# Two programs joined into one: cross-attention's first tile inside the tail of self-attention, and the third V product after the second gather group

## The reference

```python
x = layernorm(x + attn(x, W_qkv, b_qkv))
# cross-attention: K and V of the context, sums over pairs, level by level
Ks.append(0.5 * (k2[:, :, :, 0] + k2[:, :, :, 1]));  Vs.append(v2[:, :, :, 0] + v2[:, :, :, 1])
nk, nv = flatK[:, :, idx_table], flatV[:, :, idx_table]        # 12 nodes for every row
w = softmax(concat([Q.K_own, where(mask, -inf, Q.nk)]) * scale)
out = (w * concat([V_own, nv])).sum() @ Wo.T + bo
x = layernorm(x + out)
x = layernorm(x + relu(x @ w1 + b1) @ w2 + b2)
```

## Time and profile before

| | us |
|---|---|
| median of three runs | 2318.53 (2316.12 to 2335.72) |
| the profiled execution | 2324.6 |
| its span | 2322.5 |

### The profile page before, as it was taken

One profiled execution on the slowest core, in us unless ns is written; L12 is line 12 of the kernel. 1 busy time (PEld: TensorE's weight loads), 2 busy tenths in 40 slices (PEclk: granted clock), 3 DMA queues, 4 the chain that ended last, 5 costly groups with the idle time before them and its releaser, 6 DMA issues.

```text
span 2322.5 us, 34454 instructions
## 1 busy us (share of the span) xinstructions
PE 1981.8 (85%) x11744; PEld 1037.3 (45%) x11744; DVE 1846.2 (79%) x2416; ACT 1056.7 (45%) x1854; POOL 1115.6 (48%) x1132
## 2 busy tenths in 40 slices
PE   6599999999899999983248988989888899889997
PEld 2244344344344444421015555555555555555555
DVE  8489788888788998783678988888888888988850
ACT  3255555555555555552113444444444444444444
POOL 4234555544354645352536555556555456455420
PEclk9799999999999999996569999999999999999999
DMA  5334344435445443320966576666576566676520
GB/s 195 111 119 133 118 137 130 132 113 155 128 128 155 128 145 114 124 87 26 367 236 209 193 242 213 204 236 220 196 246 209 200 244 202 207 253 201 203 83 19
DMA packets 188808, 392.50 MB, mean 169 GB/s; under 512 B 20692, under 2 KB 82260, under 8 KB 188632
## 3 DMA queue, kind: packets, MB, share of 16 engines
q1 hardware_dynamic: 133336, 188.91, 25.5%
q0 software_dynamic: 55296, 201.35, 25.2%
HBM read 312.33 MB, written 77.59 MB: 168 GB/s over the span
## 4 chain that ended last, share of the span: by engine, by line
DVE 28%; DMA 10%; issue 6%; PE 4%; POOL 4%; SPq 1%; ACT 0%; DVEq 0%; ACTq 0%; POOLq 0%
DMA nb<-kv_flat,idx_rows 9%; DVE bank L1564 7%; DVE logits L1511 6%; DVE nb L1502 5%; DVE nb L1560 4%; POOL nb L1635 4%; PE bank L1239 2%; PE bank L1215 1%; DMA own<-kv_flat 1%; DVE bank L1570 1%; DVE logits L1515 1%; DVE own L1506 1%; SPq L1134 1%; DVE top L1533 1%; DVE total L1541 1%
## 5 line engine op out<-in xcount | busy, mean ns | idle before, releaser
L1635 POOL DMA_INDIRECT nb<-kv_flat,idx_rows x384 | 366.2, 954 | 137.7 <-issue 93.0
L761 DVE TENSOR_REDUCE neg_max<-rows_ps 128x1 f32<-128x512 f32 x512 | 327.0, 681 | 94.8 <-PE rows_ps L533 91.5
L1502 DVE TENSOR_TENSOR nb<-nb,bank 128x1024 f32<-128x1024 f32 x192 | 231.2, 1218 | 133.5 <-DMA nb<-kv_flat,idx_rows 118.7
L676 ACT ACTIVATE probsT<-e_ps 128x1024 f32<-128x1024 f32 x256 | 261.7, 1022 | 74.1 <-PE e_ps L565 74.0
L1663 POOL TENSOR_TENSOR nb<-nb,weights 128x1024 f32<-128x1024 f32 x96 | 182.5, 1914 | 233.2 <-DVE weights L1548 232.5
L1564 DVE TENSOR_TENSOR bank<-bank,nb 128x512 f32<-128x512 f32 x384 | 268.3, 699 | 25.1 <-DVE bank L1564 0.9
L1215 PE MATMUL bank<-x2T_hi,w_hi_sb 128*128 128x256 f16 x1024 | 280.8, 274 | 2.6 <-issue 2.6
L1215 PE MATMUL bank<-x2T_lo,w_hi_sb 128*128 128x256 f16 x1024 | 280.7, 274 | 1.5 <-issue 1.5
L1215 PE MATMUL bank<-x2T_hi,w_lo_sb 128*128 128x256 f16 x1024 | 280.5, 274 | 0.6 <-issue 0.4
L802 DVE TENSOR_TENSOR probsT<-probsT 128x2048 f32<-128x2048 f32 x96 | 229.3, 2388 | 13.7 <-ACT probsT L676 13.7
L1418 ACT ACTIVATE hid_hi<-bank,b_down 128x256 f16<-128x256 f32 x256 | 120.6, 471 | 246.0 <-remote 127.2
(11 more groups left out here) (163 smaller groups left out, 3808.7 us busy)
## 6 DMA issues: line engine op xcount, KB each, us to landing
kv_flat<-kv_nat SPq DMA_DIRECT2D x128, 256.0 KB, 2.7
own<-kv_flat SPq DMA_DIRECT2D x32, 512.0 KB
q_stack<-qk_dram SPq DMA_DIRECT2D x96, 128.0 KB, 2.8
k_stack<-qk_dram SPq DMA_DIRECT2D x96, 128.0 KB, 3.1
piece<-in_pieces SPq DMA_DIRECT2D x40, 256.0 KB, 3.0
in_sb<-in_xT SPq DMA_DIRECT2D x8, 1024.0 KB, 6.4
in_sb<-in_ctxT SPq DMA_DIRECT2D x8, 1024.0 KB, 7.8
qk_dram<-hi SPq DMA_DIRECT2D x32, 256.0 KB, 2.2
```

The source lines that it names most:

```text
L676: act.activation(probsT[:, PROBS_PLACE[quad % 2][kt], side:side + 2, :], e_ps[:], ACT.Exp, scale=1.0 / (Q_UP * K_UP)).then_inc(e_done, 1)
L761: dve.tensor_reduce(neg_max[:, g % 2, at + i:at + i + 1], rows_ps[:, i, :], AX.X, ALU.max, negate=True).then_inc(max_done, 1)
L1502: dve.tensor_tensor(kk, kk, q.unsqueeze(1).to_broadcast([P, GN, D]), ALU.mult)\
L1635: pool.indirect_dma_start(nb[:, slot(lt, g), k, :], None, kv_flat, bass.IndirectOffsetOnAxis(idx_rows[:, lt, at:at + 1], 0))\
```

## The change

There is one program, with one list of semaphores, all raised at its start. The buffers of the second part lie over those of the first that are no longer used (the function `over` makes several views of one buffer), and the PSUM banks are shared out anew. The helpers of the second part (key_sums, shift, normalise, values, gather, weight_values and so on) are the same, but for the bank's name (ROW for O) and what is shown below. What the second program did at its start is put into steps of the last batch (cross_early, called in every step of the eighth iteration) and of the tail (cross_late):

- last batch, SyncE at step 8: indices, mask, x1 of tiles 0 and 1, query weights; step 16: index arithmetic (VectorE) and copies of the identity matrix (ScalarE); steps 19 to 26: the first eight gather groups (GpSimd);
- tail: queries of tiles 0 and 1 (TensorE and ScalarE, steps 0 to 4 and 13), key sums of tile 0 (VectorE, steps 5, 7 and 9), shift at step 14, biases and the first two key groups of tile 1 at step 15, exponentials and normalised weights at steps 15 and 16; the weighted V rows of tile 0 (values(0, 0) and GpSimd's three products) at step 24, behind the normalisation of the last batch's x1; the MLP's weights from step 15 on.

In every later tile GpSimd's third V product stands behind the second gather group (`if k == 1`) and no longer behind the first.

```diff
@@ constants, buffers
+READ_CROSS, IDS_CROSS, GATHER_CROSS = 8, 16, 18
...
+inputs = sb("inputs", [P, 32 * 1024], F16)
+w_hi, w_lo, in_hi, in_lo, in_sb = over(inputs, (F16, P, 5, KC, D), (F16, P, 5, KC, D), (F16, P, 2, KC, T),
+                                       (F16, P, 2, KC, T), (F32, P, KC, T))
+nb, = over(inputs, (F32, P, SLOTS, GN, 2 * D))
...
+queries = sb("queries", [P, 8 * 1024], F16)
+q_stack, = over(queries, (F16, KS, H, T))
+w1_hi, = over(queries, (F16, P, KC, WIDTH))
...
+Q, TURN = [rows_ps[:, 0, :], e_ps[:, 0, :]], rows_ps[:, 1, :]
+PROJ = ROW = e_ps[:, 1, :]
+HB, ACC = AUX, [O, MB]
@@ sync
+    def cross_early(d):
+        if d == READ_CROSS:
+            for s in bounced:
+                sp.wait_ge(s, START + 2 * 32 * B)
+            sp.dma_start(idx_in[:], idx.rearrange("(c p) n -> p c n", p=P)).then_inc(idx_loaded, 16)
+            sp.dma_start(mask_in[:], mask.rearrange("(c p) n -> p c n", p=P)).then_inc(idx_loaded, 16)
+            sp.wait_ge(x1_stored, START + 2 * 16)
+            load_x1(0, 0)
+            load_x1(0, 1)
+            sp.wait_ge(piece_stored, START + 2 * 16 * WO_AT)
+            for dst, part in zip(wq_sb, parts):
+                sp.dma_start(dst[:], chunks(part[WQ_AT * P:WO_AT * P, :])).then_inc(wq_loaded, 16)
+
+    def cross_late(d):
+        if d == 2:
+            for s in kv_stored:
+                sp.wait_ge(s, START + 16 * B * 2 * NT // NAT)
+            load_own(0, 0)
+            for i, v in enumerate((bo, b2)):
+                sp.dma_start(bias_in[:, i, :], v.rearrange("(a n) -> a n", a=1).to_broadcast((2, D)))\
+                    .then_inc(consts2, 16)
+            sp.wait_ge(piece_stored, START + 2 * 16 * PIECES)
+            for dst, part in zip(wo_sb, parts):
+                sp.dma_start(dst[:], chunks(part[WO_AT * P:PIECES * P, :])).then_inc(wo_loaded, 16)
+        if d == 15:
+            sp.wait_ge(misc_ready, START + misc_number(B, "share", 14, False, True) + 1)
+            load_res(0, 0)
+            for dst, part in zip(w1_sb, parts):
+                sp.dma_start(dst[:].rearrange("p c (n m) -> p c n m", m=D),
+                             part[0:W2_AT * P, :].rearrange("(c n p) m -> p c n m", p=P, c=KC))\
+                    .then_inc(mlp_loaded, 16)
+            for dst, part in zip(w2_sb, parts):
+                sp.dma_start(dst[:], chunks(part[W2_AT * P:WQ_AT * P, :])).then_inc(mlp_loaded, 16)
...
             if tail:
+                cross_late(d)
                 continue
+            if last:
+                cross_early(d)
...
+    load_x1(0, 2)
+    load_x1(0, 3)
     sp.wait_ge(x1_stored, START + 16 * B * 2)
-    sp.wait_ge(piece_stored, START + 2 * 16 * PIECES)
+    load_own(0, 1)
+    round_moves(0, 0, 2)
+    round_moves(0, 1, 2)
+    round_moves(1, 0, 2)
+    with sp.Fori(1, B - 2) as b:
...
@@ tensor
+    def cross_late(d):
+        if d == 0:
+            pe.wait_ge(max_done, START + 2 * B * STEPS)
+            pe.wait_ge(minus_ready, START + 4)
+            turn_query(0, 0)
+        if d == 2:
+            pe.wait_ge(wq_loaded, START + WQ)
+            project_query(0, 0)
+        if d == 3:
+            turn_query(0, 1)
+        if d == 13:
+            pe.wait_ge(e_done, START + B * STEPS)
+            project_query(0, 1)
...
+    pe.wait_ge(aux_free, START + aux_number(B, "sum", 3, False, False, True) + 1)
+    pe.wait_ge(misc_free, START + misc_number(B, "out", 15, False, True) + 1)
+    pe.wait_ge(quad_copied, START + B * QUADS)
+    pe.wait_ge(wo_loaded, START + OUT_WEIGHTS)
+    pe.wait_ge(bias_step, START + BIAS_STEPS)
+    turn_out(0, 0)
+    turn_minus_hi(0, 0, "o")
+    project_out(0, 0)
...
@@ scalar
+    def cross_early(d):
+        if d == IDS_CROSS:
+            act.activation(minus_one[:], ident[:], ACT.Copy, scale=-1.0).then_inc(minus_ready, 1)
+            act.activation(minus_up[:], ident[:], ACT.Copy, scale=-W_UP).then_inc(minus_ready, 1)
+            act.activation(plus_one[:], ident[:], ACT.Copy).then_inc(minus_ready, 1)
+            act.activation(plus_up[:], ident[:], ACT.Copy, scale=W_UP).then_inc(minus_ready, 1)
+    def cross_late(d):
+        if d == 1:
+            turned_query(0, 0)
+        if d == 4:
+            turned_query(0, 1)
+        if d == 12:
+            act.wait_ge(consts2, START + CONSTS2)
+            act.activation(b1_down[:], b1_sb[:], ACT.Copy, scale=DOWN).then_inc(bias_step, 1)
+            act.activation(bias_in[:], bias_in[:], ACT.Copy, scale=W_UP).then_inc(bias_step, 1)
+            act.wait_ge(bias_step, START + 3)
+            act.activation(bias_hi[:], bias_in[:], ACT.Copy).then_inc(bias_step, 1)
+        if d == 15:
+            act.wait_ge(piece_stored, START + 2 * 16 * PIECES)
+            exponentials(0, 0)
+        if d == 25:
+            copy_o(0, 0)
+            turned_out(0, 0)
+            x2_sum(0, 0)
+            x2_square(0, 0)
...
@@ vector
+            if tail:
+                cross_late(d)
+            if last:
+                cross_early(d)
...
+    def attention(b, half, more, begun=False):
+
+        for lt in tiles(half)[begun:]:
...
+    def cross_early(d):
+        if d == IDS_CROSS:
+            dve.wait_ge(idx_loaded, START + 16 * 2)
...
+    def cross_late(d):
+        if d == 5:
+            key_sums(0, 0, (0, 1))
+        if d == 7:
+            key_sums(0, 0, (2, 3))
+        if d == 9:
+            key_sums(0, 0, (4, 5, 6))
+        if d == 14:
+            dve.wait_ge(hide_ready, START + 1)
+            shift(0, 0)
+        if d == 15:
+            dve.wait_ge(bias_step, START + 4)
+            dve.tensor_tensor(bias_lo[:], bias_in[:], bias_hi[:], ALU.subtract).then_inc(bias_step, 1)
+            dve.wait_ge(xb_ready, START + B * TT)
+            dve.tensor_scalar(bias_rows[:], bias_hi[:], ident[0:2, 0:1], None, ALU.mult).then_inc(bias_step, 1)
+            dve.wait_ge(bias_step, START + 6)
+            dve.scalar_tensor_tensor(out=bias_rows[:], in0=bias_lo[:], scalar=ident[0:2, 1:2],
+                                     in1=bias_rows[:], op0=ALU.mult, op1=ALU.add).then_inc(bias_step, 1)
+            key_sums(0, 1, (0, 1))
+        if d == 16:
+            normalise(0, 0)
+        if d == 24:
+            values(0, 0)
...
+    attention(0, 0, True, begun=True)
@@ gpsimd
+            if tail:
+                cross_late(d)
...
+        rows = kv_flat[0:FLAT, :] if isinstance(b, int) and b == 0 else kv_flat
...
+    def attention(b, half_, more, begun=False):
+        early = isinstance(b, int) and b == 0
+        for lt in tiles(half_)[begun:]:
...
+            for k, i in enumerate(range((lt + 1) * NG + AHEAD, (lt + 2) * NG + AHEAD)):
+                if more or i < TT * NG:
+                    gather(b, i)
+                if k == 1:
+                    weight_values(b, lt, POOL_V_GROUPS[-1:])
...
+    def cross_early(d):
+        if d == GATHER_CROSS:
+            pool.wait_ge(idx_step, START + 4)
+            pool.tensor_copy(idx_rows[:], idx_f[:]).then_inc(idx_ready, 1)
+            pool.wait_ge(idx_ready, START + 2)
+            pool.wait_ge(aux_ready, START + aux_number(B - 1, "kv", 2 * KC - 1, False, True) + 1)
+            for s in kv_stored:
+                pool.wait_ge(s, START + 16 * 2 * NT // NAT)
+        if GATHER_CROSS < d <= GATHER_CROSS + SLOTS:
+            gather(0, d - GATHER_CROSS - 1)
+    def cross_late(d):
+        if d == 24:
+            weight_values(0, 0, POOL_V_GROUPS)
+        if d == 25:
+            gather(0, NG + AHEAD)
+            gather(0, NG + AHEAD + 1)
...
-                if k == 0:
...
+    for i in range(NG + AHEAD + 2, 2 * NG + AHEAD):
         gather(0, i)
-    attention(0, 0, True)
+    for s in kv_stored:
+        pool.wait_ge(s, START + 16 * B * 2 * NT // NAT)
+    x2_rstd_of(0, 0)
+    attention(0, 0, True, begun=True)
     attention(0, 1, True)
     attention(1, 0, True)
     for b in range(1, B - 1):
```

1125 lines of the change are left out of this document (532 added, 593 removed).

## The result

The changed kernel takes 2286.5 us in the median of 4 runs (2283.1 to 2295.0), the kernel before 2317.3 in the runs beside it: a ratio of 0.985 [0.981, 0.990]. The forecast was 2281, with 2252 to 2303 as its range. The profiled execution took 2283.9 (span 2282.0), 40.7 us less than that of before.

The account below looks back on a forecast made before the run. A steady cross-attention tile was taken as bound by VectorE's work plus its wait for gathers. From the profiled 2324.6 us, +3.2 - 34.7 - 6.0 gave 2287.1; being 6.1 above the median, this made 2281, range 2252 to 2303.

Parts of the forecast that it names:

- the border: between self-attention and cross-attention: tile 1's logits hidden at 1145.3 instead of 1179.96, -34.7 us, added last-batch and tail work included.
- the third product: steady tiles, GpSimd's third V product behind gather group two: 0.2 us a tile for 30 tiles, -6.0 us, bounds -30 and +21.
- Start: before the first load: SyncE raises the second program's semaphores there too, +3.2 us.
- The last batch: gathers ahead of root and x1 splits, and competing with stores and a load: +9.5 us, bounds 3 and 15.
- the root: last reciprocal root in the last batch, behind two gather groups on GpSimd: about 3 of 5 us reach VectorE.
- The tail: self-attention's end, with key sums, queries, bias steps added: +18.5 us (11.0 plus 7.5), bounds 8.8 and 26.
- Front and tile 1: after the last normalisation: GpSimd's products and splits end at 1123.2, x1 store just in time, tile 1's logits hidden at 1145.3.
- D: stretch from the end of the last normalisation to the hiding of tile 1's logits, forecast to change by -62.6 us.
- Rival 3: border: not earlier in effect, tail products wait for gathers or queries; 2313 us with the swap, chance 0.06.
- Rival 2: border: added work in last batch and tail eats it, 34.7 us shrinks to 16.7, 2299 us; chance 0.20.
- Rival 1: steady tiles: moving the third product fills the gap in transfers, 1.0 us a tile instead of 0.2, 2257 us; chance 0.17.
- Rival 4: steady tiles: third product exposed before group five's addition, 1.92 us a tile, 57.6 us, slower at 2345 us; chance 0.07.

Follow-up runs that it names:

- the last experiment: changed kernel with index operations at 14, gathers at 24 to 31, both tail edits, two gather groups before splits, semaphores after three loads: 2267.2 us, 0.974.

## Why the prediction was right, and where it was not

The time (2286.5 against 2281) and the order of events were right, **but the time in part by luck: the border gave 10 us less than forecast and the third product 11 us more.** The start and the border were forecast at -31.5 us together. They gave -21 in the stretches and -22.0 in the runs with the product back. The third product was forecast at -6 and gave -16 to -18 in the runs.

- **Start, +3.2:** 3.4. Right, and taken back by the last experiment.
- **The last batch, +9.5:** 17, outside my bounds of 3 to 15. Of the 17, by the runs with single parts moved, some 8 to 9 are the place of the gathers in GpSimd's order: the root (3 us, right) and the x1 store, which left 11 to 12 us late, 9 of them by the gathers. The prediction had the splits "about 5 us late" and put the rest of its term down to transfers. Some 3 are the "five small index operations ... I cost them at nothing, 1 us each if the cover is gone": what covered them was no idle time but a VectorE and a GpSimd that were both at work, and they cost 5 us at once, of which the waits behind them hid a part (112.7 for 114.7, and 103.1 for 106.0). The transfers' own price is the last 5.5, against 6.5 forecast.
- **The tail, +18.5:** 15 to 20, mean 18. Up to the last reciprocal it grew by 10.3 in the means (11.0 forecast), from there to the division by 7.2 (7.5 forecast); the single terms of the 11.0 were not separated. But the last 7.5 were not a loss by themselves: taking 6 of them away gained nothing until the weights were out of the way.
- **Front and tile 1:** D was 32.8 us against 30.2 forecast: the x1 store did slip, by the 2 us of GpSimd's wait. Rival 3 (no earlier in effect) falls with D. Rival 2 (the border is eaten) was nearer on the last batch, and 10 of the 18 us that it took from the border did go.
- **The third product, -6.0:** -16 to -18 in the runs. Direction, new wait (0.48 to 0.7) and the shift of the waits were right. "I take 0.2 us, nearer zero" was too low by 0.3 to 0.4 a tile, and part of it could not be read: the first trace of the kernel before has 34.84 us a tile, the second 35.48, the changed kernel 34.63 and 34.78. Rival 1 (1.0 a tile) was as far off on the other side. Rival 4, the exposed product, doesn't hold one group later, but does two groups later (28 us, half its price).

One reading of the prediction was wrong without moving the sum. It took the 76.3% against 25.8% of the earlier trace rows to speak against equal turns of the two queues. The same rows have 675 packets against 674: the turns were equal there, and the packets were not (2.46 MB against 0.67).

The sum by what was measured is +3.4 + 17 + 18 - 59.7 - 17 = -38 us, against -39.8 in the runs of the changed kernel again, beside 18 of the kernel before. In the first set it was -30.8, where the kernel before ran 11 us faster than there. Why the steady part of the kernel before takes 34.84 us in one execution and 35.5 in others stays open, and so does why TensorE's projection is late for it a few times.

## What to carry to other kernels

Before a small operation of VectorE is costed at nothing, look at what GpSimd does in that very microsecond: two steps earlier one wait hid all five, beside GpSimd's additions they took 5 us on the spot. Before gathers are put into GpSimd's list, look at what stands behind them there: most of what they cost the last batch was a store that left late, not the transfers. When an edit shortens one stretch and the next grows by the same amount, keep it and look for the second wait; the two together were worth 8 us, each alone none. And take a second trace of the kernel before a term is built on the period of one.

## What the runs showed of the hardware

- A 128x48 operation of VectorE took 1.17 to 1.26 us beside GpSimd's additions, and 0.12 to 0.21 us without. The long ones ended with GpSimd's addition, 0.04 to 0.06 us behind it. Reductions and batch statistics beside the same additions were not longer.
- A gather issue of GpSimd took 2.83 us, not 0.94, where VectorE added probabilities (128x2048, both inputs in SBUF). Three such issues in the last batch of the changed kernel ended 0.81 to 0.83 us behind that addition. The addition itself took 2.29 and 2.38 us beside two of them. It took 3.83 (1019.11, above) where one of GpSimd's splits, 1.17 us, fell into it as well:

```profile
1020.93 2.83 POOL L1690 DMA_INDIRECT inputs<-kv_flat,idx_rows  x1 [0.16 <-issue]
```

- The mean granted clock of TensorE was lower in the last batch where TensorE waited more: 0.81 from 983 to 1045 us in the changed kernel, with TensorE busy 44.91 of 62 us, and 0.96 from 983 to 1029 in the second trace of the kernel before, busy 37.64 of 46.
- With the gathers on the other queue a 1 MB load took 12.4 us from issue to landing, and 7.4 without them.
- The semaphores of the second part, raised ahead of the first load, cost 3.4 us (7.56 against 4.15); behind the first three loads they left it at 4.13.
